# Expert pass of a two-block perceiver kernel: bias inside the gelu by chunks of 128 columns, layer norm weight and bias applied as the turned rows are copied

## The reference, cut to what matters

```python
# block 3, n runs over 4096 tokens, E = 8 experts, F = 512
z      = layernorm(x)                                   # no weight, no bias
logits = z @ Wg                                         # which 2 of 8 experts, and their gates
xn     = layernorm(z) * ln_w[e] + ln_b[e]               # per expert
h      = gelu(xn @ fc1_w[e] + fc1_b[e])                 # 128 -> 512, tanh form
y      = h @ fc2_w[e] + fc2_b[e]                        # 512 -> 128
x      = x + gates-weighted sum of the two y (times alpha[e])
# block 6: the same shape, h = gelu(z @ w1[e]), y = h @ w2[e]: no bias, no weight, exact gelu
```

## Time and profile before

| | |
|---|---|
| median of 3 runs | 1492.5 us (1491.97 to 1501.98) |
| the profiled execution | 1493.61 us; span of its instructions 1491.8 us |
| TensorE busy | 1248.6 us, 84% |
| VectorE busy | 1006.2 us, 67% |
| ScalarE busy | 836.9 us, 56% |
| GpSimd busy | 830.2 us, 56% |

### The profile page before, as it was taken

The page is one execution under the profiler, slowest core; times in us unless marked ns, Lnnn a source line. Parts: engine busy times, 40 slices in busy tenths (PEclk is TensorE's granted clock), DMA queues, the critical chain, the costliest instruction groups (busy, mean ns, idle before and its releaser), DMA issues. The chain is left out here.

```text
span 1491.8 us, 49249 instructions
## 1 busy us (share of the span) xinstructions
PE 1248.6 (84%) x15586; PEld 1084.6 (73%) x15587; DVE 1006.2 (67%) x3247; ACT 836.9 (56%) x2658; POOL 830.2 (56%) x1700
## 2 busy tenths in 40 slices
PE   3998698887489994999999999999969987369990
PEld 2777688776479993777777777777758877269990
DVE  4774378886446662788888788888759998523334
ACT  1664376664234442777777777777737776135550
POOL 2674035676646663566665666656434577736660
PEclk9997589997589996999999999999979999579995
DMA  7994651221122212322111111111000000122215
GB/s 236 328 361 145 228 157 53 69 69 44 57 64 64 66 54 65 97 65 81 35 38 50 35 53 35 41 47 32 16 16 3 17 29 27 59 56 71 67 59 176
DMA packets 93088, 121.84 MB, mean 82 GB/s; under 512 B 12402, under 2 KB 66931, under 8 KB 92947
## 3 DMA queue, kind: packets, MB, share of 16 engines
q1 hardware_dynamic: 74258, 82.70, 18.2%
q0 software_dynamic: 13312, 34.69, 6.5%
q10 hardware_dynamic: 5376, 2.63, 0.6%
HBM read 89.48 MB, written 30.49 MB: 80 GB/s over the span
## 5 line engine op out<-in xcount | busy, mean ns | idle before, releaser
L1611 ACT ACTIVATE p_prob<-six,p_nm 128x257 f32<-128x257 f32 x512 | 235.9, 474 | 121.5 <-DVE p_nm L1653 120.6
L1653 DVE TENSOR_REDUCE p_nm<-six 128x2 f32<-128x514 f32 x256 | 164.9, 685 | 36.4 <-PE six L1509 34.8
L1863 PE MATMUL bank<-sb_w,m_experts_aT 128*128 x1152 | 155.3, 278 | 2.7 <-ACT m_experts_aT L1892 2.2
L1842 POOL DMA_INDIRECT expert_outputs<-m_experts_y,m_experts_dest x144 | 142.3, 988 | 26.1 <-POOL m_experts_tiny L1841 15.8
L1879 PE MATMUL six<-m_experts_xT,m_experts_w 128*128 128x128 f32 x1152 | 156.0, 279 | 0.0
L791 POOL DMA_INDIRECT expert_inputs<-p_r_x,p_r_slot x128 | 126.2, 986 | 36.5 <-issue 35.6
L1863 PEld LDWEIGHTS bank<-sb_w,m_experts_aT 128*128 128x128 f32 x1152 | 141.3, 193 | 5.8 <-issue 5.6
L1879 PEld LDWEIGHTS six<-m_experts_xT,m_experts_w 128*128 128x128 f32 x1152 | 143.4, 196 | 0.5
L1530 PE MATMUL six<-sb_const,p_prob 128*128 128x128 f32 x1024 | 140.7, 281 | 0.0
L1390 POOL TENSOR_TENSOR p_score<-p_score,p_mx 128x512 f32<-128x512 f32 x64 | 67.1, 1049 | 124.6 <-DVE p_mx L1335 123.1
L1733 POOL TENSOR_TENSOR p_spread<-p_recip,sb_const 128x128 f32<-128x128 f32 x128 | 51.2, 400 | 150.2 <-DVE p_recip L1664 150.1
(11 more groups left out here) (293 smaller groups left out, 3504.5 us busy)
## 6 DMA issues: line engine op xcount, KB each, us to landing
ctxT_ring<-ctxT SPq DMA_DIRECT2D x32, 512.0 KB
ctxN_ring<-ctxN POOLq DMA_DIRECT2D x32, 512.0 KB, 5.5
p_ctxT<-ctxT SPq DMA_DIRECT2D x32, 512.0 KB, 3.6
m_experts_x<-expert_inputs SPq DMA_DIRECT2D x144, 64.5 KB
bd_scores<-p_rows SPq DMA_DIRECT2D x32, 256.0 KB, 2.9
p_bd<-bd_scores SPq DMA_DIRECT2D x32, 256.0 KB
sb_w<-w SPq DMA_DIRECT2D x32, 256.0 KB
p_y<-expert_outputs SPq DMA_DIRECT2D x32, 128.0 KB, 3.3
```

What stands on the lines that cost most here:

```text
L1611: last = nc.scalar.activation(prob[:, b, g, :], scores_ps[:, g, 0:CTX], ACT.Exp, bias=nm[:, b % 2, g:g + 1], accum_out=total[:, b % 2, g:g ...
L1653: nc.vector.tensor_reduce(nm[:, b % 2, g:g + 2], scores_ps[:, g:g + 2, 0:CTX], AX.X, ALU.max, negate=True).then_inc(s[most], 1)
L1842: nc.gpsimd.indirect_dma_start(m.ys_dram[:, :], bass.IndirectOffsetOnAxis(ap=dest[:, t.par:t.par + 1], axis=0), y[:, t.par, :], None).then ...
L1863: last = nc.tensor.matmul(ps[6 + t.two][:, 0:D], aT[:, t.two, f * P:(f + 1) * P], m.w2[:, DS(held[p] + f * D, D)], start=(f == 0), stop=(f ...
```

## The change

- The folding goes: steps 36 to 43 have no products with ln_b (L1217), no scaling of w1 (L1292), and VectorE no sum (L1374). Its three semaphore uses go too.
- The three loads at L1143 become one, which writes, for each expert, six columns (four of fc1_b, ln_w, ln_b) beside b2 in `m.bias`: 1024 runs of 24 bytes.
- In the experts pass of block 3: VectorE no longer computes h. Before the copy of w it copies the expert's six columns into one of four small buffers (`b1`, semaphore `columns`), and after it the destinations (moved here from ScalarE). ScalarE's copy of the turned x becomes Identity with scale ln_w and bias ln_b, one value per partition, and waits for `columns`; the gelu reads PSUM and becomes four instructions of 128 columns, each with its own bias column. TensorE's first product waits for aT (gelu) of two jobs before instead of h.
- The pass of block 6 is as before, and so is everything else.

```diff
@@ self_attention, sync @@
                     if t.n == 1:
-                        for dst, src in ((m.ln_w, "ln_wT"), (m.ln_b, "ln_bT"), (m.b1, "b1_T")):
-                            sp.dma_start(dst[:, :], m.a[src]).then_inc(s["experts_in"], 16)
+                        sp.dma_start(m.bias[:, :].rearrange("p (e f) -> p e f", e=E)[:, :, D:D + FC + 2],
+                                     m.a["expert_columns"].rearrange("p (e f) -> p e f", e=E)).then_inc(s["experts_in"], 16)
@@ self_attention, tensor @@
-                if relative and n in FOLDS:
-                    e = FOLDS.index(n)
-                    pe.wait_ge(s["experts_in"], 16 * (2 * E + 4))
-                    pe.wait_ge(s["v"], H4 * TILES)
-                    for k in range(e * FC, (e + 1) * FC):
-                        last = mm(bias_ps[:, k:k + 1], m.w1[:, k * P:(k + 1) * P], m.ln_b[:, e:e + 1],
-                                  start=True, stop=True)
-                    last.then_inc(s["b1_ps"], 1)
@@ self_attention, scalar @@
-                if relative and n - 1 in FOLDS:
-                    e = FOLDS.index(n - 1)
-                    act.wait_ge(s["b1_ps"], e + 1)
-                    w = m.w1[:, e * F:(e + 1) * F]
-                    nc.scalar.activation(w, w, ACT.Copy, scale=m.ln_w[:, e:e + 1])
@@ self_attention, vector @@
-                if relative and n == FOLDS[-1] + 1:
-                    dve.wait_ge(s["b1_ps"], E)
-                    nc.vector.tensor_tensor(m.bias[:, :].rearrange("p (e f) -> p e f", e=E)[:, :, D:D + FC],
-                                            bias_ps.rearrange("p (e f) -> p e f", f=FC),
-                                            m.b1[:, :].rearrange("p (e f) -> p e f", f=FC), ALU.add).then_inc(s["scaled"], 1)
@@ experts @@
-        w, h, aT = (sb(n, [P, 2, F]) for n in ("w", "h", "aT"))
+        w, aT, b1 = sb("w", [P, 2, F]), sb("aT", [P, 2, F]), sb("b1", [P, 4, FC + 2])
@@ experts, tensor @@
-                        pe.wait_ge(s["h" if biased else "aT"], t.before(2))
+                        pe.wait_ge(s["aT"], t.before(2))
@@ experts, scalar @@
-                    act.wait_ge(s["h" if biased else "h_ps"], t.nth())
+                    act.wait_ge(s["h_ps"], t.nth())
                     if t.past(2):
                         act.wait_ge(s["y_ps"], t.before(2))
-                    nc.scalar.activation(aT[:, t.two, :], h[:, t.two, :] if biased else ps[2 + t.two][:, :],
-                                         gelu).then_inc(s["aT"], 1)
+                    if biased:
+                        for f in range(FC):
+                            chunk = slice(f * P, (f + 1) * P)
+                            last = nc.scalar.activation(aT[:, t.two, chunk], ps[2 + t.two][:, chunk], gelu,
+                                                        bias=b1[:, t.par % 4, f:f + 1])
+                    else:
+                        last = nc.scalar.activation(aT[:, t.two, :], ps[2 + t.two][:, :], gelu)
+                    last.then_inc(s["aT"], 1)
...
-                    nc.scalar.activation(xT[:, t.two, :], ps[t.two][:, 0:P], ACT.Copy).then_inc(s["xT"], 1)
-                    act.wait_ge(x_in[t.par], t.nth_of_pair(16))
-                    if t.past(SETS):
-                        act.wait_ge(scattered[t.par], t.half * 16)
-                    nc.scalar.activation(dest[:, t.par:t.par + 1], x[:, t.par, D:D + 1], ACT.Copy).then_inc(s["dest"], 1)
+                    if biased:
+                        act.wait_ge(s["columns"], t.nth())
+                        nc.scalar.activation(xT[:, t.two, :], ps[t.two][:, 0:P], ACT.Identity,
+                                             scale=b1[:, t.par % 4, FC:FC + 1],
+                                             bias=b1[:, t.par % 4, FC + 1:FC + 2]).then_inc(s["xT"], 1)
...
@@ experts, vector @@
                     if t.past(2):
                         dve.wait_ge(s["h_ps"], t.before(2))
+                        if biased and t.past(4):
+                            dve.wait_ge(s["aT"], t.before(4))
+                    if biased:
+                        nc.vector.tensor_scalar(b1[:, t.par % 4, :], m.bias[:, DS(held[p + SECOND - FIRST] + D, FC + 2)],
+                                                1.0, None, ALU.mult).then_inc(s["columns"], 1)
                     nc.vector.tensor_scalar(w[:, t.two, :], m.w1[:, DS(held[p + SECOND - FIRST], F)], 1.0, None,
                                             ALU.mult).then_inc(s["w"], 1)
-                t = at(2)
-                if t.live and biased:
-                    dve.wait_ge(s["h_ps"], t.nth())
-                    if t.past(2):
-                        dve.wait_ge(s["aT"], t.before(2))
-                    by_chunk = lambda ap: ap.rearrange("p (f n) -> p f n", f=FC)
-                    nc.vector.tensor_tensor(by_chunk(h[:, t.two, :]), by_chunk(ps[2 + t.two][:, :]),
-                                            m.bias[:, DS(held[p + SECOND - 2] + D, FC)].unsqueeze(2).broadcast_to(
-                                                [P, FC, P]), ALU.add).then_inc(s["h"], 1)
+                    if biased:
+                        dve.wait_ge(x_in[t.par], t.nth_of_pair(16))
+                        if t.past(SETS):
+                            dve.wait_ge(scattered[t.par], t.half * 16)
+                        nc.vector.tensor_copy(dest[:, t.par:t.par + 1], x[:, t.par, D:D + 1]).then_inc(s["dest"], 1)
```

More of the change, by code:

```diff
@@ L1089, in self_attention @@
         "shifted", "probs", "pT", "o_ps", "recip", "o", "oT_ps", "oT", "y_ps", "xb", "zres", "ones",
-        "experts_in", "b1_ps", "scaled", "negative")}
+        "experts_in", "negative")}
     bd_in = [m.sem(name + "_bd_in_a"), m.sem(name + "_bd_in_b")]
@@ L1101, in self_attention @@
     y_ps = quad[:, 0, P:2 * P]
-    FOLDS = range(36, 36 + E)
     with ExitStack() as own, nc.Block() as block:
@@ L1115, in self_attention @@
                           ps[7][:, 192:224], s["o_ps"], s["zT_ps"])
-        bias_ps = ps[6][:, 0:E * FC]
         wq = m.w["Wq_a" if relative else "w_q"][:, :]
@@ L1149, in _ @@
                 each_step(TILES + 2, work)
-                sp.wait_ge(s["experts_in"], 16 * (2 * E + 4))
+                sp.wait_ge(s["experts_in"], 16 * (2 * E + 2))
             routing.sp_gaps(sp)
@@ L1781, in lay_out_experts @@
         "w1_1": first(f["L1_ffn_w1"]), "w2_1": second(f["L1_ffn_w2"]),
-        "ln_wT": f["L0_ffn_ln_w"].T, "ln_bT": f["L0_ffn_ln_b"].T,
-        "b1_T": f["L0_ffn_fc1_b"].reshape(E, FC, P).transpose(2, 0, 1).reshape(P, E * FC),
+        "expert_columns": np.concatenate([f["L0_ffn_fc1_b"].reshape(E, FC, P).transpose(2, 0, 1),
+                                          f["L0_ffn_ln_w"].T[:, :, None], f["L0_ffn_ln_b"].T[:, :, None]], 2).reshape(P, -1),
         "b2": np.tile(f["L0_ffn_fc2_b"].reshape(1, E * D), (P, 1)), "alpha": np.tile(f["L0_ffn_alpha"][None], (P, 1)),
@@ L1792, in experts @@
     nc, ps = m.nc, m.ps
-    s = {n: m.sem(name + "_" + n) for n in ("xT_ps", "xT", "w", "h_ps", "h", "aT", "y_ps", "y", "dest", "go")}
+    s = {n: m.sem(name + "_" + n) for n in ("xT_ps", "xT", "w", "columns", "h_ps", "aT", "y_ps", "y", "dest", "go")}
     SETS = 8
@@ L1898, in work @@
                         act.wait_ge(s["h_ps"], t.before(2))
-                    nc.scalar.activation(xT[:, t.two, :], ps[t.two][:, 0:P], ACT.Copy).then_inc(s["xT"], 1)
-                    act.wait_ge(x_in[t.par], t.nth_of_pair(16))
-                    if t.past(SETS):
-                        act.wait_ge(scattered[t.par], t.half * 16)
-                    nc.scalar.activation(dest[:, t.par:t.par + 1], x[:, t.par, D:D + 1], ACT.Copy).then_inc(s["dest"], 1)
+                    if biased:
[3 more added lines that the diff above has]
+                                             bias=b1[:, t.par % 4, FC + 1:FC + 2]).then_inc(s["xT"], 1)
+                    else:
+                        nc.scalar.activation(xT[:, t.two, :], ps[t.two][:, 0:P], ACT.Copy).then_inc(s["xT"], 1)
+                    if not biased:
+                        act.wait_ge(x_in[t.par], t.nth_of_pair(16))
+                        if t.past(SETS):
+                            act.wait_ge(scattered[t.par], t.half * 16)
+                        nc.scalar.activation(dest[:, t.par:t.par + 1], x[:, t.par, D:D + 1], ACT.Copy).then_inc(s["dest"], 1)
             over_tiles(act, STAGES, work, HALVES, SETS)
@@ L2028, in build @@
         m.gates = sb("gates", [P, TILES, TOPK])
-        m.b1, m.ln_w, m.ln_b = sb("b1", [P, E * FC]), sb("ln_w", [P, E]), sb("ln_b", [P, E])
         m.job_row, m.job_expert = sb("job_row", [P, JOBS], I32), sb("job_expert", [P, AROUND + JOBS + AROUND], I32)
```

## The result

| | before | after |
|---|---|---|
| median | 1494.11 us of 16 runs (1484.6 to 1501.98) | 1487.82 us of 16 runs (1482.0 to 1494.55) |
| ratio | | 0.9962, 95% interval 0.9944 to 0.9981: 5.7 us less (2.8 to 8.4) |
| the profiled execution | 1493.61 us | 1485.09 us, span 1483.0 us |
| experts of block 3, first load of x to the next pass's first load | 160.10 us | 155.97 us |
| the same for block 6 | 152.78 us | 151.74 us |

The ratios in this document are of runs at the kernel's usual granted clock; the one run outside it, 1582.28 us at 0.78 in the later best_order, is left out of its ratio.

What follows compares the result with a forecast made beforehand. Passes between barriers bound the kernel, TensorE and register-load stalls the block 3 experts: 142.65 + 0.7 + 0.5 = 143.9 us from 149.87, folding and loads 0, so 1492.5 - 6.0 = 1486.5 us; range 1484.0 to 1492.5.

Steps and rivals of the forecast that it cites:

- The place of the loss, and the mechanism: Block 3 experts: after each register load, VectorE's late h delays gelu and second product, 0.96 us per eight jobs.
- Bounds: 0, and 0.96 ... I take 0.1 for each of seven: Block 3 experts: stall left after each of seven register loads, 0.1 us each, 0.7 us in all.
- The working's own sum: Block 3 experts after a load: two-job loop of 3.2 us plus y 0.76 late, 3.96 against 3.79 us.
- the wait for columns takes the place of the wait for h: Rival, block 3 experts: late y still costs 0.96 us per load, gain 0, 1492.5 us; stall kept partly or wholly 0.18.
- The drain, +0.5: End of block 3's experts pass: the last gelu takes 1.15 instead of 0.60 us, once, +0.5 us.
- Prices: Block 3 experts: gelu chunk 0.367 us, four 1.15, turned x 0.47, small copies 0.2 each.
- Tables, and ScalarE as the bound: Rivals, block 3 experts: two table loads per job, 1629 us, chance 0.02; ScalarE becomes the bound, 1512 us, chance 0.05.
- The folding, 0 us: End of relative pass: GpSimd's scatters hide the folding, removal gains 0; rival of 17 us gained there, chance 0.04.
- 4.5 us of slack: End of relative pass: last slots ready at 390.7, GpSimd needs them at about 395.2, so the folding is hidden.
- The loads, 0 us: Bias loads: one issue replaces three and costs SyncE nothing more; 0 us, bounds 0 to +2 us.

Runs made afterwards that it cites:

- best_order: Changed kernel with only the copy of the six columns issued ahead of y, third chip: 1522.77 us, ratio 0.9941 to the kernel before.
- y_last: Changed kernel with VectorE's y moved behind the columns, w and the destinations in the experts passes: 1493.7 us.
- columns_first: Changed kernel with only the copy of the six columns issued ahead of y, first chip: 1485.86 us.
- gelu_in_one: Changed kernel with the four gelus as one instruction of 512 columns with one bias column, the other three left out: 1491.0 us.
- folding_back: Changed kernel with the folding's products, scalings and sum put back, results unused, second chip: 1530.52 us.
- before_w_first: Kernel before the change with VectorE's w ahead of y, second chip: 1542.48 us, against 1527.33 for the kernel before.
- loads_twice: Changed kernel with VectorE's register loads in block 3 written twice; the second was dropped, VectorE's program identical to the change's; second chip: 1527.47 us.
- dest_on_act: Changed kernel with the copy of the destinations given back to ScalarE, second chip: 1520.01 us.
- before_copy: Kernel before the change, unedited, profiled on the third chip: 1531.11 us.
- folding_again: Changed kernel with the folding's work put back, results unused, third chip: 1525.66 us, ratio 0.9964 to the kernel before.
- loads_again: Changed kernel with VectorE's register loads written twice, in effect the change once more, third chip: 1528.13 us.

## Why the prediction was right, and where a step failed

**The whole: right, in part by luck.** 5.7 us less on the first chip, 6.0 forecast, with the time inside the range. But the pass itself gained 4.1, and the interval (2.8 to 8.4) holds both numbers.

**The place of the loss, and the mechanism: right.** The pass of block 6 was the yardstick, and the wait for h behind each register load was the loss. h's wait is gone, the eight jobs went from 16.12 to 15.62 us, and y_last and columns_first reach block 6's 15.17 us (to 0.02) with all of the bias work in place.

**"Bounds: 0, and 0.96 ... I take 0.1 for each of seven": the step that failed.** It measured 0.46. Worked out from the starts of y, the eight periods have 0, 0.25, 0.53 and then five times 0.45 or 0.46 us over 15.17, 3.05 in all, where the sum had 0.7. With block 6's 142.65 this gives 145.70, against 145.78 measured and 143.9 forecast. Three things made the difference. The working's own sum was 3.96 - 3.79 = 0.17, and it took 0.1. The same chain, read from the second product of 475.70 in the timeline after, is longer than 3.96: y starts 1.93 us into the job (1.85 forecast), the columns are ready at 478.11 (0.48 later, 0.46 forecast), the turned x starts only at 478.23, a hand-over of 0.12 us that the working had at nothing, the gelus start at 478.59 and end at 479.72, and the second product starts at 479.86. That is 4.16 us against 3.79, so 0.37 instead of 0.17. And the next second product (481.85) comes another 0.09 us late, 1.99 us instead of 1.90, which the working didn't have at all. The rival "the wait for columns takes the place of the wait for h" named this very mechanism at the full 0.96; it happened, at half that price, in the stretch that the text left between the two. Rival and forecast weren't two cases here but two ends of one.

**The drain, +0.5: right at the last y, and in part hidden behind it.** The last two y of the pass start 1.52 us apart, in block 6 1.03, and in gelu_in_one, with its shorter gelu, 1.11. But the last scatter ends 1.71 us after the start of the last y, in block 6 2.05, as there it stands behind the scatter before it: GpSimd gives back 0.34. In all, the pass is 3.13 us longer than block 6's 142.65: +2.96 in the eight periods (block 6 has 0.07 over eight times 15.17 itself), +0.63 in the last seven distances, -0.34 at the end and -0.12 before the first y.

**Prices.** The chunk was taken at 0.367, four at 1.15; they measured 0.371 and 1.13 to 1.14. The Trainium skill (ScalarE: Activation LUTs, What ACT_TABLE_LOAD costs) gave 0.387 and 1.27. The row of the trace was the better price. For one ACTIVATE of all 512 columns with one bias column the same line of the page comes to 0.28 + 512 x 0.833 ns = 0.71 us, an estimate; gelu_in_one measured 0.68, and 0.60 was measured without the bias column, in block 6, near the page's 0.093 us for a pointer operand. The turned x measured 0.46 (0.47 taken). The small copies measured 0.175 and 0.144 (0.2 taken for each).

**Tables, and ScalarE as the bound: fell as reasoned.** One table load in the pass. ScalarE is busy 109.59 of 145.78 us, 1.52 us a job of 2.02, where 1.4 was worked out. That Identity lies beside the gelu in one table, which only the Trainium skill stated (the same page, Table sets: the hidden batching unit), this trace now shows: 72 Identity copies between 288 gelus, and one load.

**The folding, 0 us: right on the first chip, and narrower than the text made it.** The scatters take 29.89 us from first to last after (29.93 before), and the first load of x comes 9.50 us behind the last of them (9.53 before). TensorE and VectorE did get free (the job table ends at 397.07 instead of 402.90), and then waited, as forecast. But "4.5 us of slack" was a property of one chip: on two others a stall of ScalarE and VectorE used it up and left the scatters 4.2 to 4.9 us later, in all four kernels with folding and in none of the four without. What that is worth in the end isn't settled. On the second chip the whole relative pass took 265.20 and 264.19 us with folding (folding_back, before_w_first), 257.41 and 255.96 without (loads_twice, dest_on_act), 7 to 9 us more. On the third it took 258.69 and 261.06 with (before_copy, folding_again), 259.24 and 259.40 without (loads_again, best_order), since the stretch ahead of these scatters was 3 to 5 us shorter there with folding. These are single executions, and on the first chip kernels without folding already ranged from 242.33 to 251.96.

**The loads, 0 us: no sign against it.** The one load took SyncE 0.62 us to issue, the three 2.22 together. The relative pass up to the 24th scatter from the end took 204.08 us before and 204.21 after.

## What to carry to other kernels

When a wait is moved to another instruction, don't price it by a loop's length alone: walk the chain behind the disturbance in the engines' own order, give each hand-over between two engines its price, keep the sum that comes out, and ask of each instruction ahead of the awaited one whether anybody needs it sooner. Here a copy of 0.17 us standing behind a y that nobody was in a hurry for cost 0.46 us per eight jobs, and issuing it first took all of it back. Work that "hides" with a few microseconds of slack hides on the chip where it was measured; on two other chips a stall had used the slack up.

## What the runs showed of the hardware that had not been expected

- Two other chips ran every kernel of this study some 35 us longer. By passes, the kernel before took, on the third chip and the first, 258.69 instead of 243.54 us in the relative pass, 234.42 instead of 220.98 in the causal one and 165.36 instead of 160.10 in the experts of block 3, and nearly the same in cross attention (517.99 against 519.44) and in block 6 (153.44 against 152.78). So it isn't a slower clock over the whole. The cause isn't shown.
- In block 3's experts on these chips VectorE and ScalarE now and then start late together with everything done that they are known to wait for: in best_order the gelus start at 497.42 and the columns at 497.62, though the product both wait for had ended at 496.61. There y waited 9.8 us in all for what the profile calls "issue" (in columns_first, the same kernel on the first chip, at most 1.1), and eight jobs took, behind the first eight, 15.9 to 16.6 us instead of 15.2; in the same execution block 6 kept 15.16 to 15.28. The stall of 1.38 us in before_w_first is of this kind. The 8 us stall in the relative pass looks alike. No run here tells the cause.
- A busy TensorE can be a waiting one: 31.25 of 31.25 us busy, with 0.46 us lost in every 15.62. The loss sits in matmul groups of 1.15 us that are 1.06 elsewhere. Count jobs per time, not busy time.
